# Where the attention residual is added to its PSUM bank in an eight-chunk RWKV kernel, and when GpSimd makes the second half's k*v

## The reference

```python
xn = _ln(x, ln1_w, ln1_b)
...
def step(s, rkvw):
    r_t, k_t, v_t, w_t = rkvw
    a = k_t[:, :, :, None] * v_t[:, :, None, :]
    out = jnp.einsum('bhk,bhkd->bhd', r_t, u * a + s)
    return (a + w_t[:, :, :, None] * s, out)
...
x = x + att * g @ Wo.T
xn2 = _ln(x, ln2_w, ln2_b)
...
rr = jax.nn.sigmoid(xr @ ffn_Wr.T)
kk = jnp.square(jax.nn.relu(xk @ ffn_Wk.T))
x = x + rr * (kk @ ffn_Wv.T)
```

## Time and profile before

| | us |
|---|---|
| median of three runs | 692.4 |
| the three runs | 690.88, 692.4, 697.16 |
| the profiled execution, its time | 689.89 |
| its span, first to last instruction | 688.0 |

### The profile page before, as it was taken

How to read it: one execution, slowest core, us unless ns; L and a number is a source line. 1 busy time by engine, 2 the same in 40 slices (tenths; PEclk the granted TensorE clock), 3 DMA queues, 4 the chain that set the end, 5 groups by cost and what they waited for, 6 DMA issues and landing times.

```text
span 688.0 us, 9610 instructions
## 1 busy us (share of the span) xinstructions
PE 613.5 (89%) x2694; PEld 332.2 (48%) x2694; DVE 574.1 (83%) x902; ACT 390.5 (57%) x933; POOL 294.1 (43%) x210
## 2 busy tenths in 40 slices
PE   8999999979787859899899989989988998995896
PEld 5666666647232224354445435344543534443475
DVE  2999999973568898978997997899799789959944
ACT  3888888853443354567365455737546464353343
POOL 1111363002035293475639428464851946590020
PEclk9999999999999999999999999999999999998699
DMA  2343222201270841456267055526706540670020
GB/s 68 121 124 105 83 72 61 83 13 31 77 168 0 154 92 31 80 135 124 31 153 143 10 106 131 99 30 152 152 4 127 131 74 4 149 153 30 0 31 30
DMA packets 42444, 57.87 MB, mean 84 GB/s; under 512 B 4978, under 2 KB 25106, under 8 KB 42418
## 3 DMA queue, kind: packets, MB, share of 16 engines
q1 hardware_dynamic: 33008, 46.77, 29.6%
q0 software_dynamic: 9104, 10.77, 8.9%
q10 hardware_dynamic: 306, 0.02, 0.0%
HBM read 16.13 MB, written 7.86 MB: 35 GB/s over the span
## 4 chain that ended last, share of the span: by engine, by line
PE 29%; DVE 17%; issue 11%; POOL 7%; ACT 4%; DMA 1%; SPq 1%; DVEq 0%; POOLq 0%; ACTq 0%
PE ps_a L793 9%; DVE state L1459 8%; PE ps_c L878 6%; PE ps_c L793 3%; POOL x L683 2%; POOL state L656 2%; DVE vb L1464 2%; PE ps_att L858 2%; DVE x L1419 2%; PE ps_a L816 1%; PE ps_a L821 1%; DVE sx L1537 1%; DMA vb<-v 1%; PE ps_c L931 1%; POOL xn L646 1%
## 5 line engine op out<-in xcount | busy, mean ns | idle before, releaser
L683 POOL TENSOR_TENSOR x<-x,xn 128x1024 f32<-128x1024 f32 x35 | 86.2, 2471 | 151.0 <-DVE x L1419 151.0
L1459 DVE TENSOR_TENSOR_SCAN state<-ps_w,state 128x512 f32<-128x512 f32 x128 | 145.8, 1200 | 0.2
L793 PE MATMUL ps_a<-x,wsq 128*128 128x512 f32 x256 | 119.3, 610 | 10.1 <-POOL x L683 7.5
L656 POOL TENSOR_TENSOR state<-vb,k 128x2016 f32<-128x2016 f32 x23 | 105.3, 4577 | 27.0 <-DVE state L1446 10.4
L1464 DVE TENSOR_TENSOR vb<-state,r 128x2048 f32<-128x2048 f32 x32 | 86.1, 2692 | 1.7
L793 PEld LDWEIGHTS ps_a<-x,wsq 128*128 128x128 f32 x256 | 48.5, 195 | 68.9 <-issue 59.4
L1419 DVE SCALAR_TENSOR_TENSOR x<-ps_a,vec,sx 128x512 f32<-128x512 f32 x80 | 56.2, 745 | 27.7 <-PE ps_a L816 15.9
L310 ACT ACTIVATE probs<-ps_f,negmax 128x256 f32<-128x256 f32 x128 | 59.0, 473 | 1.9 <-DVE negmax L364 1.1
L816 PE MATMUL ps_a<-mix_t,w 64*128 64x512 f32 x128 | 47.6, 634 | 9.8 <-ACT mix_t L1161 7.1
L1117 ACT ACTIVATE zn<-wyz,rs 128x256 f32 (+1 forms) x60 | 31.1, 594 | 22.5 <-POOL rs L640 22.5
L374 DVE TENSOR_SCALAR probs<-probs,rowinv 128x256 f32<-128x256 f32 x128 | 41.8, 369 | 2.2
(11 more groups left out here) (213 smaller groups left out, 1259.3 us busy)
## 6 DMA issues: line engine op xcount, KB each, us to landing
vb<-v SPq DMA_DIRECT2D x120, 256.0 KB, 5.5
x<-in_x SPq DMA_DIRECT2D x32, 128.0 KB, 2.1
c<-in_ctx SPq DMA_DIRECT2D x32, 128.0 KB, 2.3
wyz<-in_x POOLq DMA_DIRECT2D x7, 512.0 KB, 5.9
out<-wyz SPq DMA_DIRECT2D x7, 512.0 KB, 7.4
out<-sx POOLq DMA_DIRECT2D x7, 512.0 KB, 6.4
vb<-v SPq DMA_DIRECT2D x16, 128.0 KB, 2.4
wsq<-in_wsq POOLq DMA_DIRECT2D x7, 256.0 KB, 3.2
```

The lines of the kernel that those rows point to most:

```text
L656: nc.gpsimd.tensor_tensor(st[q][:, :, :, 1:L], src[:, :, :, 0:L - 1], wide(k[p][h][:, :])[:, :, :, 0:L - 1], ALU.mult).then_inc(kv_at(n, h ...
L683: nc.gpsimd.tensor_tensor(x5[j % 2][:, :, :], x5[j % 2][:, :, :], xn[:, :, 1:L1], ALU.add).then_inc(x5_ready, 1)
L793: mm = nc.tensor.matmul(bank[:, :], wsq[:, weight, c, P * o:P * o + P], src(c), start=(c == 0), stop=(c == EC - 1))
L1459: nc.vector.tensor_tensor_scan(row, w[h][:, :], row, 0.0, ALU.mult, ALU.add).then_inc(scanned, 1)
```

## The change

- ScalarE's `c_x1` is gone, in the bodies and in the last pass.
- `c_out` on TensorE has no identity product any more; the bank holds only `att * g @ Wo.T`.
- A new function `c_res` on VectorE, called right before the moments, adds each bank (o0, o1) to its two slices of `wyz` in place and counts `x1_ready`.
- In `body` on GpSimd, `b_kv(n,p,1,0)` stands ahead of `add_x(n+1,0)`, and behind a new wait, `hold_gated(n-1)`, for both `ag_ready` of `c_gn(n-1)`. The last pass keeps its order on GpSimd.

```diff
--- before.py
+++ after.py
@@ -675,6 +675,9 @@
                 pool.wait_ge(last_ln, 2 * i + 1)
                 nc.gpsimd.tensor_tensor(rs2[:, 1, cut], ve2[:, 1, cut], rs2[:, 0, cut], ALU.mult).then_inc(last_ln, 1)
 
+            def hold_gated(n):
+                pool.wait_ge(ag_ready, n * 2 + 2)
+
             def hold(n):
                 pool.wait_ge(bonus_ready, n * 2 + 2)
 
@@ -708,8 +711,9 @@
                 q = 1 - p
                 prev(n - 1, sx2_ready, xprev2, t["prev0"], xn2)
                 prev(n + 1, sx_ready, xprev, t["prev1"], xn)
+                hold_gated(n - 1)
+                b_kv(n, p, 1, 0)
                 add_x(n + 1, 0)
-                b_kv(n, p, 1, 0)
                 if z:
                     z_add(n + 2)
                 add_x(n + 1, 1)
@@ -886,11 +890,9 @@
                     bank = c_bank(n, f"o{i}")
                     for m in range(2):
                         lo = P * (2 * i + m)
-                        z = wyz[:, bass.ds(n * TILES + 2 * i + m, 1), :].rearrange("p a f -> p (a f)")
-                        nc.tensor.matmul(bank[:, E * m:E * m + E], ident, z, start=True, stop=False)
                         for c in range(EC):
                             mm = nc.tensor.matmul(bank[:, E * m:E * m + E], ag[:, c, lo:lo + P], wsq[:, WO, c, :],
-                                                  start=False, stop=(c == EC - 1))
+                                                  start=(c == 0), stop=(c == EC - 1))
                     mm.then_inc(c_done, 1)
 
             def c_turn(n):
@@ -1207,12 +1209,6 @@
                     act.wait_ge(var_ln, n * 2 + h + 1)
                     nc.scalar.activation(sq[h][:, :], sq[h][:, :], ACT.Exp, scale=-0.5).then_inc(gn_rstd, 1)
 
-            def c_x1(n):
-                for i in range(2):
-                    act.wait_ge(c_done, c_at(n, f"o{i}"))
-                    nc.scalar.activation(wyz[:, bass.ds(n * TILES + 2 * i, 2), :], cb(f"o{i}")[:, :].rearrange("p (m f) -> p m f", m=2),
-                                         ACT.Copy).then_inc(x1_ready, 1)
-
             def c_xn2(n):
                 for c in range(EC):
                     act.wait_ge(c_done, c_at(n, f"T{c}"))
@@ -1316,7 +1312,6 @@
                 a_tanh(n + 1)
                 if z:
                     a_bias(n + 2)
-                c_x1(n - 1)
                 state_column(n, 1, 0)
                 state_column(n, 1, 1)
                 a_w(n, 1)
@@ -1529,6 +1523,12 @@
             def c_x1(n):
 
                 moments(n, x1_ready, n * 2 + 2, st2b, mv2, ve2, st2, mv2_s, ln2_var)
+
+            def c_res(n):
+                for i in range(2):
+                    dve.wait_ge(c_done, c_at(n, f"o{i}"))
+                    x1 = wyz[:, bass.ds(n * TILES + 2 * i, 2), :]
+                    nc.vector.tensor_tensor(x1, cb(f"o{i}")[:, :].rearrange("p (m f) -> p m f", m=2), x1, ALU.add).then_inc(x1_ready, 1)
 
             def c_shift(n):
                 dve.wait_ge(xn2_ready, n * 2 + 2)
@@ -1590,6 +1590,7 @@
                 a_mod(n + 1, 0, 0, 1)
                 a_mod(n + 1, 1, 0, 1)
                 b_scan(n, p, 0, 1)
+                c_res(n - 1)
                 c_x1(n - 1)
                 b_scan(n, p, 1, 0)
                 c_shift(n - 1)
```

## The result

| | before | after |
|---|---|---|
| median, us | 692.4 (5 runs) | 707.41 (5 runs) |
| lowest to highest | 690.77 to 697.16 | 706.36 to 712.69 |
| ratio | | 1.022, interval 1.019 to 1.026 |
| profiled execution, span | 688.0 | 711.1 |

Slower by 15 us, where 1.1 us over the old median was forecast and 701 was the upper end of the range.

What follows compares the result with a forecast made beforehand. VectorE was taken to bound gated attention to `c_shift`, TensorE the stretch from the keys product through gate projection. Bodies 1 to 5 -0.4, body 6 +1.5, last pass +0.8: +1.9 us on 691.6, forecast 693.5 us, range 687 to 701.

Steps and rivals of the forecast that it cites:

- the fourth: VectorE's part (0,1) product, asking during GpSimd's `z_add` issue, runs at once, 393.63 to 395.92, 1.39 us shorter.
- VectorE bounds the stretch from gated attention to `c_shift`: In each body the chain from gated attention to `c_shift` runs on VectorE, without gaps; TensorE already waits there.
- TensorE's identity products are worth nothing there: Removing them from `c_out` frees 1.76 us a pass on TensorE, counted as no gain in six passes.
- rival 1: TensorE is the bound everywhere, so 12.3 us go, giving 679; chance 0.1.
- rival 4: TensorE's clock falls once a body from added idle time: +3 to +9 us, about 699; chance 0.05.
- TensorE's busy time falls by some 12 us: Sign of being right: TensorE's busy time falls by some 12 us and its idle time grows as much.
- The additions at 1.31 us: VectorE's two new additions before the moments cost +1.31 us per pass, with no wait for GpSimd's `add_x`.
- rival 3: VectorE's additions take turns with `add_x(1)`: +2.2 us in five bodies, 704.5 us in all; chance 0.05.
- `b_kv` ahead of `add_x`, -1.39 us in bodies 1 to 5: GpSimd's new order lets VectorE's part (0,1) product run unheld, 1.39 us shorter in each of bodies 1 to 5.
- Rival 2: GpSimd's `add_x(1)` gets the turn before VectorE's product: some +1.7 us in bodies 1 to 5, 702.4 us; chance 0.07.
- Body 6: Without `z_add`, the product waits for `add_x(1)`: +0.15 us, plus 1.31 for the additions, +1.5 us.
- Last pass: GpSimd's old order; additions from 629.76, moments at 631.07 in place of 630.28: +0.8 us.

Runs made afterwards that it cites:

- hold_add: Changed kernel with one more GpSimd wait: `add_x(1)` starts only after the product of part (0,1) is made; 690.37 us against 691.8, ratio 0.999.
- before_hold_add: Kernel before, identity products and ScalarE copies kept, plus `hold_gated`, GpSimd's new order and `add_x(1)` waiting for the part (0,1) product; 684.05 us, ratio 0.988.
- residual_only: Residual half: changed kernel with GpSimd's old order, keeping VectorE's additions, without identity products or ScalarE copies; 700.36 us, ratio 1.013.
- order_only: Kernel before with only `hold_gated` and GpSimd's new order; identity products and ScalarE copies stay; 700.46 us, ratio 1.012.
- the wide copy: Changed kernel with a 128 x 512 SBUF copy on GpSimd after `z_add`, then `add_x(1)` waiting for the product; 692.84 us, before 695.57.

## Why the prediction was wrong, point by point

The step that failed is the fourth: that a product which asks during the issue of `z_add` runs at once.

- **VectorE bounds the stretch from gated attention to `c_shift`**: right. `hold_add` and `before_hold_add` move it by just what VectorE's rows move by, less the 0.31.
- **TensorE's identity products are worth nothing there**: right, rival 1 is out. In `hold_add`, with the identity products gone and the product at 2.29 us, bodies 1 to 5 are 59.02 us apart; with TensorE as the bound they would have come down by 1.76. The size was a little less than I estimated: TensorE's busy time in a body at clock 1.00 falls from 54.88 to 53.29 us, 1.6 and not 1.76. What the sum put at nothing is that TensorE's idle time can cost something: the clock. In the residual half it took 1.7 us in all (rival 4, priced at 3 to 9), in the bodies of the whole change nothing. I took from the Trainium skill (TensorE: Matmul & The Clock Gate, Why this matters for your kernels) that a longer gap than the new ones was needed, and reckoned with pieces of 1.1 us. The pieces became 2.53 us and 1.05 in the residual half, and there the runs show the lower level in four bodies of six. Those gaps too are shorter than the Trainium skill asks for there, and the measurement decides.
- **TensorE's busy time falls by some 12 us**, which I gave as a sign of being right: it rose, from 613.5 to 617.3 us, 4.0 of it ahead of the first body. In the bodies it is 327.4 us where it was 327.1, since the lower clock made the products that were left longer. In `hold_add` it falls by 9.8 us, to 603.7.
- **The additions at 1.31 us**: right, 13.47 against 12.16 in `residual_only`; they take no turn with `add_x` (0.68 us each beside it), so rival 3 is out. The rule of the Trainium skill (SBUF — State Buffer, Who interferes with whom) for an instruction with one SBUF input agrees with this.
- **`b_kv` ahead of `add_x`, -1.39 us in bodies 1 to 5**: this step failed. The term measured +1.63 in the body of n = 2, and 1.5 to 1.8 in the five. The times of GpSimd's line held (337.17, 341.60, 343.72 and 344.55, which is 1.7, 6.1, 8.2 and 9.0 us after the start of the gated attention; foreseen 1.5, 5.9, 8.0 and 8.9), and so did the product's request, in the middle of `z_add`'s issue. What fell is the inference from GpSimd being in the DMA's issue at that moment to the product running. I drew it from 395.17, where the product had been waiting since 393.63 and got its turn at `b_kv`'s end, ahead of an `add_x` in line. A product that asks after GpSimd has started on the DMA, with `add_x(1)` in line behind it without a wait, finds the turn gone: -1.39 became 5.31 - 3.68 = +1.63, an error of 3.0 us a body, 15 us in five.
- **Rival 2** named this outcome, with the wrong trigger (that `z_add` take under 0.5 us; it took 0.83 as before) and too low a price: 1.7 us a body, 702.4 us in all, where it was 2.94 a body. It let `add_x(1)` run from before the product's request; but `add_x(1)` ends at 347.22, as if its 2.17 us began only when the issue was over (343.72 + 1.30 = 345.02, an estimate).
- **Body 6**: product +0.15 foreseen, 3.83 against 3.69 found; to the moments 13.61 against 12.16, +1.45. **Last pass**: 652.10 and 653.41 after a gated pair at 643.37, 10.04 against 9.26, +0.78; 0.8 foreseen.
- **The sum**: with +2.94 in place of -0.08, 5 x 2.94 + 1.45 + 0.78 = 16.9 us. Measured, the six passes of the profile give 15.8 us and the last one 0.8, the medians 15.0 in all.

## What to carry to other kernels

An engine pair that takes turns needs an order by semaphore wherever both ask at nearly the same time; a start time in the profile doesn't tell who has the turn, and a gap of 0.3 us on paper is no order. One wait on the engine with slack (`hold_product`) was worth some 16 us here: 15.0 over the kernel before without it, 1.4 under it with it. Where an edit pays on one engine and charges another, run each half alone: here the one that charges was the bound, and the version without it is the fastest. And an engine that gets more idle time may run its next work at a lower clock, so look at the granted clock where you take work away.

## What the runs showed of the hardware that was not expected

- GpSimd holds VectorE's two-input product off for an instruction that stands behind a DMA issue up to 0.5 us before its shown start (344.07 against 344.55; with the wide copy to 0.55 us after the issue's start, in five bodies of five). With a wait for the product in between it does not (2.29 us), nor with an instruction of 128 x 1 and that wait. The trace has no event for the taking of the turn. The wide copy, 0.61 us alone, ends some 0.45 us behind the product, so it was not done when it let the product in; what holds the product stays open.
- GpSimd's first instruction behind a DMA issue is 0.50 to 0.54 us longer (2.67 for 2.17, 5.02 for 4.48; a memset of 128 x 1 0.60 for 0.10).
- TensorE's clock fell to the lower level around 2.53 us without work and up to 1.05 more in bodies 2 to 5 of `residual_only` (projection to v 6.25, 6.62, 6.74, 5.16 us), and not in bodies 1 and 6 (3.69 us) with the same gaps. In `hold_add` it fell once in six bodies, with pieces of 0.58 and 1.35 us (projection 5.39 us in body 2). In `order_only` it fell in three of the five bodies with a piece of 2.3 to 2.6 us. With pieces of 0.80 and 1.05 us, as before, it stayed at 1.00 in all six. What decides among equal gaps stays open.
- A TENSOR_SCALAR of 128 x 4 with its one tensor input in SBUF took 0.60 us beside `add_x` and ended 0.04 us after it, and 0.17 with GpSimd idle (last pass before and after). The additions, with one input in a bank, were not longer beside `add_x`.
